# Layer 0 of an attention stack: loads as one long piece per partition, issued from two queues

## The reference

```python
def layernorm(x, g, b):
    mu = jnp.mean(x, axis=-1, keepdims=True)
    var = jnp.mean(jnp.square(x - mu), axis=-1, keepdims=True)
    return (x - mu) * jax.lax.rsqrt(var + EPS) * g + b

x1 = layernorm(modality1, ln1_g, ln1_b)      # modality1 = layernorm(x)
x2 = layernorm(modality2, ln2_g, ln2_b)      # modality2 = the context
q = x1 @ Wq + bq
k = x2 @ Wk + bk
v = x2 @ Wv + bv
scores = jnp.einsum('bqe,bke->bqk', q, k) * scaling
attn = jax.nn.softmax(scores, axis=-1)
ctx = jnp.einsum('bqk,bke->bqe', attn, v)
return ctx @ Wo + bo
```

## Time and profile before

| | us |
|---|---|
| median of 3 runs | 2025.12 |
| lowest and highest run | 2020.41, 2026.07 |
| the profiled execution: span, first to last instruction | 2025.9 |
| PE busy | 1815.4 (90%) |
| DVE busy | 1478.2 (73%) |
| ACT busy | 1047.6 (52%) |
| POOL busy | 710.6 (35%) |

### The profile page before, as it was taken

The page is one execution under the profiler, slowest core; times in us unless marked ns, Lnnn a source line. Parts: engine busy times, 40 slices in busy tenths (PEclk is TensorE's granted clock), DMA queues, the critical chain, the costliest instruction groups (busy, mean ns, idle before and its releaser), DMA issues. The chain is left out here.

```text
span 2025.9 us, 36437 instructions
## 1 busy us (share of the span) xinstructions
PE 1815.4 (90%) x11942; PEld 1605.4 (79%) x11942; DVE 1478.2 (73%) x3467; ACT 1047.6 (52%) x2347; POOL 710.6 (35%) x742
## 2 busy tenths in 40 slices
PE   3776999999999999999757999999968999999698
PEld 3654999989899899899736888888856888888587
DVE  4658778777777777778676666666677777777786
ACT  1325656555655555556454555555512666666321
POOL 0311202020202020202003566666642667677442
PEclk9988999999999999999978999999979999999799
DMA  5010000000000000000001111111000000000011
GB/s 151 1 73 24 9 1 12 1 11 0 11 0 11 0 11 0 3 0 1 1 0 63 53 52 52 52 52 64 32 1 22 11 11 20 11 10 3 22 53 39
DMA packets 17564, 47.80 MB, mean 24 GB/s; under 512 B 2174, under 2 KB 11327, under 8 KB 15808
## 3 DMA queue, kind: packets, MB, share of 16 engines
q1 hardware_dynamic: 16032, 29.45, 4.8%
q10 hardware_dynamic: 1440, 17.31, 2.5%
HBM read 45.83 MB, written 0.92 MB: 23 GB/s over the span
## 5 line engine op out<-in xcount | busy, mean ns | idle before, releaser
L1241 ACT ACTIVATE a_pH<-bank 125x512 fp32r<-125x512 f32 (+1 forms) x384 | 203.5, 543 | 272.6 <-PE bank L170 192.8
L170 PE MATMUL bank<-a_pH,a_head_vH 125*128 125x256 f32 (+2 forms) x960 | 318.5, 332 | 14.4 <-DVE a_pL L1937 10.9
L1312 DVE TENSOR_TENSOR a_pL<-bank,a_pH 125x512 fp32r<-125x512 f32 (+1 forms) x384 | 235.4, 623 | 100.3 <-ACT a_pH L1241 96.7
L170 PE MATMUL bank<-a_pH,a_head_vL 125*128 125x256 f32 (+2 forms) x960 | 278.2, 290 | 0.0
L170 PE MATMUL bank<-a_pL,a_head_vH 125*128 125x256 f32 (+2 forms) x960 | 278.2, 290 | 0.0
L1626 POOL TENSOR_TENSOR a_prob<-a_prob,a_rinv 112x750 f32<-112x750 f32 x128 | 183.3, 1437 | 166.4 <-DVE a_rinv L1927 166.1
L1098 POOL TENSOR_TENSOR a_head_oH<-a_o,ones 128x256 fp32r<-128x256 f32 (+1 forms) x24 | 16.4, 684 | 624.2 <-DVE a_o L1321 624.2
L1288 DVE TENSOR_SCALAR_CACHE_REDUCE a_prob<-bank 128x500 f32<-128x500 f32 x336 | 222.9, 677 | 16.7 <-PE bank L170 7.9
L1006 DVE TENSOR_REDUCE a_head_v_sum<-bank 125x256 f32<-125x512 f32 x288 | 194.3, 688 | 42.6 <-PE bank L914 28.5
L976 POOL TENSOR_TENSOR a_head_vL<-a_head_v_sum,a_head_vH 125x256 fp32r<-125x256 f32 x288 | 203.1, 735 | 58.7 <-ACT a_head_vH L962 57.8
L1142 PE MATMUL bank<-ident,a_prob 128*125 128x128 f32 x1344 | 201.5, 274 | 6.6 <-ACT a_prob L1226 4.4
(11 more groups left out here) (373 smaller groups left out, 4686.4 us busy)
## 6 DMA issues: line engine op xcount, KB each, us to landing
a_expert<-in_f_w ACTq DMA_DIRECT2D x8, 2048.0 KB, 8.5
a_head_w_raw<-in_a_w SPq DMA_DIRECT2D x24, 384.0 KB, 3.2
f_raw<-in_f_w SPq DMA_DIRECT2D x9, 513.0 KB, 3.7
f_quant_raw<-in_f_w SPq DMA_DIRECT2D x3, 1024.0 KB, 6.4
a_head_wo_raw<-in_a_wo SPq DMA_DIRECT2D x24, 128.0 KB, 2.1
a_v<-in_ctx_rows SPq DMA_DIRECT2D x4, 562.5 KB
a_raw_main<-in_ctx_cols SPq DMA_DIRECT2D x1, 1500.0 KB, 10.8
a_raw_tail<-in_ctx_cols SPq DMA_DIRECT2D x2, 750.0 KB, 15.4
```

Of the source, the lines that this page charges most:

```text
L170: last = pe.matmul(out, a, b, start=start and n == 0, stop=stop and n == len(terms) - 1)
L1241: act.activation(pH[:, c % RING, 0:wide], TB[c % 4][0:KB, 0:wide], ACT.Copy).then_inc(t_high, 1)
L1312: dve.tensor_tensor(pL[:, c % RING, 0:wide], TB[c % 4][0:KB, 0:wide], pH[:, c % RING, 0:wide].bitcast(F32), ALU.subtract).then_inc(t_done, 1)
```

## The change

Three things change, all in layer 0. The context rows, x and the weights a_wq and a_wo are laid out by the host so that what one partition gets lies in one piece in DRAM; the context rows also lie in one piece in the buffer, since `ctx_rows` is now the front part of `v` with tiles 192 floats apart instead of 256. Of the four row loads the first and third stay on the SP queue, the second and fourth go to the scalar queue, between a_cols and a_wkv. The four constants move from the SP queue to the scalar queue, behind a_wkv. The instructions of PE, DVE and POOL are the same in kind, size and order.

```diff
-        ctx_rows = v[:, :, 0:DC]
+        ctx_rows = v[:].rearrange("p t d -> p (t d)")[:, 0:KTILES * DC].rearrange("p (t d) -> p t d", d=DC)
...
         @block.sync
         def _(sp):
-            c_dram = dram["ctx_rows"].rearrange("(j p) d -> p j d", p=KB)
-            for n in range(LOADS):
+            for n in range(0, LOADS, 2):
                 sp.dma_start(ctx_rows[:, n * PER:(n + 1) * PER, :],
-                             c_dram[:, n * PER:(n + 1) * PER, :]).then_inc(ctx_loaded[n], 16)
-            sp.dma_start(s.x[:], dram["x"].rearrange("(t p) d -> p t d", p=P)).then_inc(x_loaded, 16)
-            sp.dma_start(s.ident[:], dram["ident"]).then_inc(small_loaded, 16)
-            sp.dma_start(s.ones[:], dram["ones"]).then_inc(small_loaded, 16)
-            sp.dma_start(s.earlier[:], dram["earlier"]).then_inc(small_loaded, 16)
-            sp.dma_start(rows[:], dram["a0_rows"]).then_inc(small_loaded, 16)
+                             dram["ctx_rows"][:, n * PER:(n + 1) * PER, :]).then_inc(ctx_loaded[n], 16)
+            sp.dma_start(s.x[:], dram["x"]).then_inc(x_loaded, 16)
             for w, name in ((w_q, "a0_wq"), (w_o, "a0_wo")):
-                sp.dma_start(w[:], dram[name].rearrange("(k p) n -> p k n", p=P)).then_inc(w_loaded, 16)
+                sp.dma_start(w[:], dram[name]).then_inc(w_loaded, 16)
...
         @block.scalar
         def _(act):
             act.dma_start(cols[:], dram["a0_cols"]).then_inc(wkv_loaded, 16)
+            for n in range(1, LOADS, 2):
+                act.dma_start(ctx_rows[:, n * PER:(n + 1) * PER, :],
+                              dram["ctx_rows"][:, n * PER:(n + 1) * PER, :]).then_inc(ctx_loaded[n], 16)
             act.dma_start(wkv[:], dram["a0_wkv"]).then_inc(wkv_loaded, 16)
+            act.dma_start(s.ident[:], dram["ident"]).then_inc(small_loaded, 16)
+            act.dma_start(s.ones[:], dram["ones"]).then_inc(small_loaded, 16)
+            act.dma_start(s.earlier[:], dram["earlier"]).then_inc(small_loaded, 16)
+            act.dma_start(rows[:], dram["a0_rows"]).then_inc(small_loaded, 16)
...
-    a = {"x": i["x"].reshape(TOK, D)}
+    a = {"x": tiled(np, i["x"].reshape(TOK, D))}
     rows = i["ctx_768"].reshape(NK, DC)
-    a["ctx_rows"], a["ctx_cols"] = rows, rows.T
+    a["ctx_rows"], a["ctx_cols"] = rows.reshape(KTILES, KB, DC).transpose(1, 0, 2), rows.T
...
     for n in "qo":
-        a["a0_w" + n] = i["L0_xattn_W" + n]
+        a["a0_w" + n] = tiled(np, i["L0_xattn_W" + n])
```

## The result

The changed kernel takes 2037.78 us (median of 4 runs, 2037.0 to 2039.09), the kernel before beside it 2023.35 us (4 runs, 2020.41 to 2026.07). The ratio is 1.0079, with a 95% interval from 1.0063 to 1.0094: slower by 12.7 to 19.0 us. Forecast were 2032 us, in a range from 2016 to 2042, with slower as the likeliest sign; as a step over the kernel before, +6.2 us by the forecast's sum and +14.4 by the medians.

A forecast was written before the change was run, and what follows sets the result against it. The start waits for rows on about five DMA engines, and POOL and DVE exclude each other. Constants +3.4, collision +10.9, less 8.1 old PE idle: +6.2 us; leaning to the larger spread, 2032 us, range 2016 to 2042.

The forecast's parts named there:

- Five engines, before and after: Row loads: 125 partitions use five of 16 DMA engines whichever queue issues them, at a share of 0.34.
- Rivals 2 and 3: Rows leave the five engines: 2016 us, chance 0.18; also with POOL's cut where DVE needs no lock: 2008, 0.03.
- rival 1: No change within 6 us: loads end clean, POOL meets only part of the L117s; about +2, 2027 us; chance 0.21.
- Late constants set the transposes: Start of PE's transposes: constants land last, at 38.3 us, so transposes start 3.4 us later than before.
- crowded end: Last loads land at 41.0 us if loads hinder each other while the eleven engines work; +8.9 us in all.
- crowding factor of 1.39: Loads beside each other: 7.30 us between landings against 5.26; stretches the eleven engines' 14.1 us to 19.6.
- wkv at 28: wkv waits behind ACT's row loads and lands at 28; bias matmuls until 32; on the path if at 36.
- Rows at 26: Last row loads: ready at 26 us, giving the first normalised tile at 32.5, ahead of the constants.
- Six more issues on ACT done by 5 us: ACT's added load issues end by about 5 us, before its first work at 32; no cost.
- POOL's cut 8.2 us earlier: POOL's cut of the transposed context: raw loads land at 38.3 instead of 46.4, so it starts 8.2 us earlier.
- the collision: POOL's cut and DVE's L310 and group 3 of L117 exclude each other: 10.9 us lost, less 8.1 old idle time.
- everything after it follows unchanged: After the last L296: the +6.2 us there carries through unchanged to the end.

The follow-up runs named there:

- e8: The changed kernel with x, a_wq, a_wo and the transposed context issued only once all four row loads have landed: 2018.82 us, ratio 0.9989 to the kernel before.
- e4: The changed kernel with row loads on 128 partitions, three of them zeros that are never read: 2018.69 us, ratio 0.9972 to the kernel before.
- e9: The changed kernel with each row load cut into two DMAs, over 120 and 5 partitions: 2023.34 us, ratio 1.0009 to the kernel before.
- e11: e7 with all four row loads, then the constants, then the rest on SP; only a_cols and wkv on the scalar queue: 2000.40 us, ratio 0.9904.
- e12: The changed kernel with the two 64-partition tail loads made into one of 128 partitions: 2034.91 us, ratio 1.0056 to the kernel before.
- e6: The changed kernel with POOL's cut held until x's seven tiles are through both layer norms: 2029.89 us, ratio 1.0038 to the kernel before.
- e7: The changed kernel with row loads on 128 partitions and POOL's cut held until x's layer norms are done: 2008.49 us, ratio 0.9936 to the kernel before.
- e10: e7 with the constants ahead of the row loads on the scalar queue and wkv behind them: 2016.79 us, ratio 0.9974 to the kernel before.
- e2: The change's queues and order with the old layout, in pieces of 768 and 1024 bytes: 2047.24 us, ratio 1.0117 to the kernel before.
- e3: The changed kernel with the constants and wkv ahead of the row loads on the scalar queue: 2044.74 us, ratio 1.0095 to the kernel before.

## Why the prediction was right, and what in it was not

**Five engines, before and after: right.** The rows stay on them with two queues and long pieces (e8, 129 GB/s at 0.32), and leave them with 128 partitions (e4) or 120 (e9). The Trainium skill's rule on the number of engines (DMA: Bandwidth & Descriptors, Why a DMA increments its semaphore by 16 and not by 1) agrees with all three: 125 gives 5, 120 gives 15, 128 gives 16; a share of 1.03 in e9 can't tell 15 from 16. The prediction has "whichever queue issues it"; that the engines are always the lowest-numbered ones the Trainium skill says, in the same section, only of queues like those of SP and the scalar engine, the two used here. Rivals 2 and 3, which needed rows off the five engines, are out; so is rival 1, which needed large pieces to crowd less than the 1.39 of the kernel before, and they crowded more.

**Late constants set the transposes: right, the size was not.** 38.3 us was forecast for all last loads, with 41.0 as the crowded end; they came at 45.8 and 46.6. The term that was mis-sized is the crowding factor of 1.39, from two gaps between landings in the kernel before. The forecast had the eleven engines done after 14.1 us of work stretched by it, so at 21.6. In after they are done at about 27: (27 - 2) / 14.1 is a factor of 1.77. With it the forecast's own formula gives 2 + 25 + 19.4 = 46.4, where 46.6 was measured. So close a hit is luck in part: by the slices the five engines moved some 2090 kB after 27 us at 108 GB/s, where the formula has 2300 at 118.5. And taking the middle between 35.5 and 41.0 had no row behind it: the crowded case was the one that the trace of before showed.

**What the factor is made of** is known for one part. The tails are loads on 64 partitions, and while they move, all 16 engines are busy at about half of the 400 GB/s of e4, or less: 193 to 162 GB/s in after, 205 and 210 in e4, 192 to 228 in e11. e12 takes them away, and the eleven engines are done by 24 us instead of 27. (It also reads a doubled copy in DRAM where the two tails read the same bytes twice; the two aren't separated.) The trace of the kernel before has it too, 167 and 168 GB/s from 36 to 42 us, and I had not read it there. The Trainium skill has a rule for this (SBUF — State Buffer, Door 1: The DMA port swizzle): partitions 0 to 63 reach only half of the ports on which DMAs write. Runs here agree with half the rate; that ports are the reason is not shown by them. What is left, 230 to 280 GB/s in e12 where e4 has 400, goes with loads of 125 partitions beside loads of 128. It isn't the five engines as such, since e9, off them, is as slow, 221 to 262 GB/s until 14 us, and back at 408 once its row loads are through. Nor is it the row loads by themselves: alone, in e8, they have 25.8 GB/s for each engine, and what follows them has 446 on all 16. It takes both kinds at once. Why stays open.

**wkv at 28: too early.** It came at 35.65, near the 36 from which the forecast called it a matter of the path. The bias matmuls behind it were done 6.78 us before a_rows let PE go, so it cost nothing.

**Rows at 26: too early,** 33.70 in fact, and free for the same reason: PE waits for the constants.

**Six more issues on ACT done by 5 us: wrong, without a price.** The last took 8.18 us, and ACT was free at 13.79, long before its first work on the rows at 37.33.

**POOL's cut 8.2 us earlier: wrong.** It began at 46.26, outside of the 35 to 41 that I had named as the sign, as was the last L291 at 82.35 (72 to 78 were named). But the forecast had the cut and the transposes start together, at 38.3, and they did, at 46.26 and 46.60; that is why the collision came out nearly as worked out. L305 (L310 in the text) was held until POOL's second instruction ended, and group 3 of L117 took 9.17 us (10.2 forecast). The Trainium skill's rule on two SBUF inputs (SBUF — State Buffer, Who interferes with whom), which no row of before could show, agrees with the trace: 5.19 us beside POOL, 1.22 without it (e6). Forecast for the collision were 10.9 - 8.1 = +2.8 us, measured are +2.2. The total at the last L291 was forecast as +6.2 and is +13.8. The late constants alone are 8.25 more than forecast (11.65 instead of 3.4), the collision 0.6 less. Of the 13.8, 1.7 come back before the next part, where the step "everything after it follows unchanged" failed by that much.

**2037.78 us in a range up to 2042: right in part by luck.** The forecast had +8.9 at its crowded end and reached up to +17 only by another path, SP's pieces delaying wkv to 38 so that the transposes wait for the bias matmuls. The +13.8 and +14.4 lie between the two, and it was not wkv that took them there but constants still later than the crowded end.

So the sign and the mechanism were right, and a size was off by more than a factor of two. The profiles differ by 11.4 us and the medians by 14.4, because the profiled execution of before is a long one: a time stands some 1.8 us over its span in the runs of after, so this one, with a span of 2025.9 us, took some 2027.7, above all four runs of before. What makes one run take 2020 us and another 2026 stays open.

## What to carry to other kernels

Before the shape of the pieces comes the number of partitions: pad a load of 125 to 128 (e4), and make two loads of 64 into one of 128 (e12), where the bytes allow it. Keep the large loads on one queue in the order in which they are needed (e11 against e7, 8.1 us); here a second queue added no engines, and whatever stood last on it ended about as late as the whole. A load that frees another engine's work (here POOL's cut) has a best time of its own, and a wait on the work that it disturbs can be worth more than getting it there early.

## What the hardware showed that I had not expected

- Two queues look served by pieces, not by bytes: 1124 packets with 1.98 MB and 996 with 5.67 MB end within 1 us of each other. In e10 a row load takes 18.4 us on the scalar queue, behind small loads, and 4.6 in front on SP's. In e2 the queues end close together too, at 48.7 and 47.6, with 2374 and 3270 packets; counted for one of the five engines, these are some 360 and 410 (an estimate from the 1500 row pieces of each queue). The Trainium skill (DMA: Bandwidth & Descriptors, Queues, rings and completion order) says that an engine goes round the queues by whole packets of several descriptors; how many pieces one turn takes isn't shown here.
- An issue can hold the engine that makes it: that of a 128 KB load stood 8.18 us on ACT (after), that of wkv 12.61 us (e2). That a full queue is the reason is likely, not shown.
- DVE instructions of 0.18 us are held beside POOL as well: L101 took 3.51 us and L106 2.12 (e3).
